# First attention layer: scores of two heads side by side in two 64-row tiles, and values projected with standing weights

## The reference

```python
# NH = 32 query heads, KVH = 8 key/value heads, GROUPS = 4, HD = 16
q = hidden @ Wq + bq;  k = ctx @ Wk + bk;  v = ctx @ Wv + bv
scores = einsum('bkgld,bksd->bkgls', q, k) * HD ** -0.5 + mask
attn = softmax(scores);  out = einsum('bkgls,bksd->bkgld', attn, v)
x = layer_norm(out @ Wo + bo + hidden) * gamma + beta
# then two cross-attention layers of 16 heads of 128, and an MLP of 2048
```

## Time and profile before

| | us |
|---|---|
| median of 3 runs | 2617.61 |
| lowest, highest | 2616.01, 2618.43 |
| profiled execution, first to last instruction | 2614.3 |
| loop of the first layer, batch 0 (38.59 to 282.59) | 244.0 |
| loop of the first layer, batch 1 (1337.68 to 1581.70) | 244.0 |

### The profile page before, as it was taken

One profiled execution on the slowest core, in us unless ns is written; L12 is line 12 of the kernel. 1 busy time (PEld: TensorE's weight loads), 2 busy tenths in 40 slices (PEclk: granted clock), 3 DMA queues, 4 the chain that ended last, 5 costly groups with the idle time before them and its releaser, 6 DMA issues.

```text
span 2614.3 us, 48985 instructions
## 1 busy us (share of the span) xinstructions
PE 2580.6 (99%) x17560; PEld 2145.5 (82%) x17560; DVE 1730.6 (66%) x2636; ACT 1504.9 (58%) x2356; POOL 1311.1 (50%) x746
## 2 busy tenths in 40 slices
PE   8999999999999999999999999999999999999999
PEld 6777788888888888888877777888888888888887
DVE  7999775656657666665279996665666576666541
ACT  5999555555545555545459994555554455554543
POOL 1244246666543666654613432466655546665644
PEclk9999999999999999999999999999999999999999
DMA  7312025345322435442472110344544143553521
GB/s 202 101 51 68 34 68 130 99 115 134 104 75 76 122 98 126 128 103 80 153 154 83 54 65 33 90 108 110 130 113 120 53 99 99 125 129 102 131 72 65
DMA packets 88386, 261.81 MB, mean 100 GB/s; under 512 B 20112, under 2 KB 33696, under 8 KB 81840
## 3 DMA queue, kind: packets, MB, share of 16 engines
q1 hardware_dynamic: 86336, 258.83, 37.3%
q10 hardware_dynamic: 1904, 0.98, 0.2%
HBM read 135.45 MB, written 6.83 MB: 54 GB/s over the span
## 4 chain that ended last, share of the span: by engine, by line
PE 88%; DVE 4%; issue 2%; ACT 2%; DMA 2%; POOL 1%; SPq 1%; DVEq 0%; POOLq 0%; ACTq 0%
PE ps_m L1059 21%; PE ps_t L1059 18%; PE ps_s L1059 15%; PE ps_m L1316 6%; PE ps_t L1316 6%; PE ps_t L1191 6%; PE ps_m L1206 5%; PE ps_s L1175 4%; PE ps_m L1191 3%; POOL pT_lo L524 1%; SPq L442 1%; PE ps_m L1249 1%; PE ps_m L1069 1%; DMA pT_lo<-pb 1%; ACT p L850 1%
## 5 line engine op out<-in xcount | busy, mean ns | idle before, releaser
L524 POOL TENSOR_TENSOR pT_lo<-pT_lo,pT_hi 128x1024 fp32r<-128x1024 f32 x220 | 529.2, 2406 | 501.7 <-ACT pT_hi L710 496.4
L710 ACT ACTIVATE pT_hi<-pT_lo 128x1024 fp32r<-128x1024 f32 x224 | 237.8, 1061 | 327.6 <-DMA pT_lo<-pb 327.6
L850 ACT ACTIVATE p<-ps_s,nm 128x1024 f32<-128x1024 f32 x256 | 284.7, 1112 | 203.4 <-DVE nm L1752 202.7
L1749 DVE TENSOR_REDUCE nmx<-ps_s 128x1 f32<-128x1024 f32 x256 | 309.7, 1210 | 121.6 <-PE ps_s L1059 121.6
L1059 PE MATMUL ps_s<-kT,qT 128*128 128x512 f32 x1536 | 383.9, 392 | 0.1
L1768 DVE STREAM_TRANSPOSE pb<-p 128x1024 f32<-128x1024 f32 x224 | 278.1, 1242 | 106.2 <-ACT p L850 101.7
L1059 PEld LDWEIGHTS ps_s<-kT,qT 128*128 128x128 f32 x1536 | 281.3, 188 | 55.6 <-ACT p L850 1.0
L1674 DVE CUSTOM_DVE_ANT_0 sm<-ps_s,mask 128x1024 f32<-128x1024 f32 x256 | 309.7, 1211 | 5.6 <-ACT p L804 2.2
L804 ACT ACTIVATE p<-sm,nm 128x1024 f32<-128x1024 f32 x256 | 293.7, 1147 | 33.3 <-DVE nm L1674 30.7
L1059 PE MATMUL ps_t<-ctxT,wa 128*128 128x512 f32 x1080 | 256.0, 390 | 0.0
L1059 PE MATMUL ps_m<-hT,wa 128*128 128x512 f32 x1008 | 243.7, 393 | 0.7 <-ACT g L1021 0.7
(11 more groups left out here) (176 smaller groups left out, 4671.7 us busy)
## 6 DMA issues: line engine op xcount, KB each, us to landing
pT_lo<-pb SPq DMA_DIRECT2D x896, 128.0 KB, 2.3
stg_qk<-in_wqk SPq DMA_DIRECT2D x40, 1024.0 KB, 7.5
stg_vo<-in_wo SPq DMA_DIRECT2D x48, 512.0 KB, 3.5
wob<-in_wo SPq DMA_DIRECT2D x32, 512.0 KB, 3.6
stg_vo<-in_wv SPq DMA_DIRECT2D x32, 512.0 KB, 3.6
q_stack<-scr_q SPq DMA_DIRECT2D x48, 128.0 KB, 4.2
st_ctx<-in_ctxT SPq DMA_DIRECT2D x8, 512.0 KB, 6.6
bv_row<-scr_bv SPq DMA_DIRECT2D x32, 128.0 KB, 5.7
```

What stands on the lines that cost most here:

```text
L524: return nc.gpsimd.tensor_tensor(out, x, f32(hi), ALU.subtract)
L710: return nc.scalar.activation(out, in_, ACT.Copy)
L850: nc.scalar.activation(p[t % 2][:], ps_s[t % 2][:], ACT.Exp, bias=nm[:, i:i + 1], scale=SCALE1, accum_out=sums[:, i:i + 1]).then_inc(exp_d ...
L1749: nc.vector.tensor_reduce(nmx[:, i:i + 1], ps_s[t % 2][:], AX.X, ALU.max, negate=True)\
```

## The change

Scores: keys and queries are now kept as two float32r parts, 48 rows for a head instead of 96. Two heads lie in one stack, at rows 0 to 47 and 64 to 111, and `scores0(r)` makes steps 2r and 2r+1 together: four matmuls of 512 columns, two for each bank of `ps_s`, alternating between the two tiles. It waits for the maxima of both steps before. The loops of TensorE, ACT and VectorE go by pairs of steps. The two heads of a pair belong to different key/value heads; `v32` gets a third block of 16 columns, and `w0o` another order of rows. VectorE makes one low part instead of three operations with two bfloat16 parts. Values: `add_v` projects them as the keys, with the weights stationary and 512 tokens moving, 24 matmuls per batch; ACT adds the bias into `vT0`, TensorE turns it in eight transposes, and VectorE copies it to `v32` in two copies.

```diff
-Q_ORDER = (0, 0, 1, 1, 0, 2)
-K_ORDER = (0, 1, 0, 1, 2, 0)
+Q_ORDER = (0, 0, 1)
+K_ORDER = (0, 1, 0)
+TILE = 64
+PAIRS0 = STEPS0 // 2
-        v32 = sb("v32", [P, ST, KVH, 2 * HD], F32)
+        v32 = sb("v32", [P, ST, KVH, 3 * HD], F32)
-        bank_of_half = [h % 2 if h < 2 * UNIT else h % 3 for h in range(2 * STEPS0)]
+        bank_of_half = [h % 2 if h < 2 * UNIT else (0, 1, 2, 0, 2, 1, 0, 2)[h % 8] for h in range(2 * STEPS0)]
...
@@ scalar, set-up
+                for i in range(2):
+                    act.wait_ge(v0_filled, 2 * b + i + 1)
+                    nc.scalar.activation(vT0[:, i * 512:(i + 1) * 512], ps_t[i][:], ACT.Identity, scale=1.0,
+                                         bias=cols0[:, 5:6]).then_inc(v0_biased, 1)
                 for k in range(2):
                     act.wait_ge(scr_k_out[k], 16 * (b + 1))
-                    stack_k(act, k, slice(0, 2), stack_in)
+                    stack_k(act, k, slice(0, 1), stack_in)
@@ scalar, loop
-                for t in range(STEPS0):
+                for t in range(1, STEPS0, 2):
+                    copied0(t - 1, 0)
                     copied0(t, 0)
                     if t + 2 < STEPS0:
+                        exp0(t + 1)
                         exp0(t + 2)
@@ tensor, set-up
                 for c in range(CT):
                     pe.wait_ge(in_hi, b * (CT + 2) + 1 + c + 1)
-                    for i in range(2):
-                        add_k(i, c, 0, 0, start=c == 0)
-                        add_k(i, c, 1, 0)
+                    for add in (add_k, add_v):
+                        for i in range(2):
+                            add(i, c, 0, 0, start=c == 0)
+                            add(i, c, 1, 0)
...
-                project_v0(0)
+                finish_v(0)
...
                 project_q0(0)
-                for i in range(1, 4):
-                    project_v0(i)
...
+                finish_v(1)
...
+                for i in range(2):
+                    pe.wait_ge(v0_biased, 2 * b + i + 1)
+                    for s in range(4):
+                        st = 4 * i + s
+                        mm = nc.tensor.transpose(ps_t[i][:, s * P:(s + 1) * P], vT0[:, st * P:(st + 1) * P], ident[:])
+                    mm.then_inc(v0_turned, 1)
@@ tensor, loop
+                def scores0(r):
+                    kp, lt = divmod(2 * r // UNIT, LT)
+                    if r >= 1:
+                        pe.wait_ge(max0_done, t0 + 2 * r)
                     for n in range(2):
+                        for e in range(2):
+                            rows = slice(TILE * e, TILE * e + STACK)
+                            mm = nc.tensor.matmul(ps_s[e][:, n * 512:(n + 1) * 512],
+                                                  q_stack[rows, kp * GROUPS + r % GROUPS, lt * P:(lt + 1) * P],
+                                                  k_stack[rows, kp, n * 512:(n + 1) * 512],
+                                                  start=True, stop=True)
+                            if n == 1:
+                                mm.then_inc(s0_filled, 1)
...
-                for t in range(1, STEPS0):
+                for r in range(1, PAIRS0):
+                    t = 2 * r + 1
...
+                    if r + 1 < PAIRS0:
+                        scores0(r + 1)
+                    turned0(t - 1)
                     turned0(t)
...
-                    if t >= GROUPS and t % 2 == 1:
+                    if t >= GROUPS:
                         for i in (t % GROUPS - 1, t % GROUPS):
                             values0(t // GROUPS * GROUPS - GROUPS, i)
@@ vector, set-up
+                def low_part(i):
+                    dve.wait_ge(wide_done, b * 6 + i + 1)
+                    apart()
+                    nc.vector.scalar_tensor_tensor(out=parts[i % 3][:, 1, :], in0=ps_m[i % 2][:], scalar=column0(i),
+                                                   in1=f32(parts[i % 3][:, 0, :]), op0=ALU.add, op1=sub)\
+                        .then_inc(part_done, 1)
...
@@ vector, loop
-                for t in range(STEPS0):
+                for t in range(1, STEPS0, 2):
...
                     if t + 2 < STEPS0:
+                        maxima0(t + 1)
                         maxima0(t + 2)
+                    copied0(t - 1, 1)
                     copied0(t, 1)
...
-                    if t % UNIT == GROUPS and t > UNIT:
+                    if t % UNIT == GROUPS + 1 and t > UNIT:
                         normalised(t // UNIT - 1)
```

More of the change, by code:

```diff
@@ L136, in build @@
         at[0] += 128
-        q_stack = sb("q_stack", [STACK, NH0, L], BF16)
-        k_stack = sb("k_stack", [STACK, KVH, S], BF16)
-        v32 = sb("v32", [P, ST, KVH, 2 * HD], F32)
+        q_stack = sb("q_stack", [P, NH0 // 2, L], F32R)
+        k_stack = sb("k_stack", [P, KVP, S], F32R)
+        v32 = sb("v32", [P, ST, KVH, 3 * HD], F32)
         mask = sb("mask", [P, LT, S], F32)
@@ L344, in turned_bank, with stack_rows, stack_k @@
             return ps_s[c // 2][:, c % 2 * 512:(c % 2 + 1) * 512]
-        def stack_k(engine, i, kvs, done):
+        def stack_rows(e, j):
+            return slice(TILE * e + HD * j, TILE * e + HD * j + HD)
+        def stack_k(engine, i, kps, done):
             for j in range(len(K_ORDER)):
-                src = scr_k[i, :, K_ORDER[j], :].rearrange("(a e) n -> e a n", e=HD)
-                engine.dma_start(k_stack[HD * j:HD * j + HD, kvs, i * 512:(i + 1) * 512], src[:, kvs, :])\
-                    .then_inc(done, 16)
+                src = scr_k[i, :, K_ORDER[j], :].rearrange("(k e d) n -> e d k n", e=2, d=HD)
+                for e in range(2):
+                    engine.dma_start(f32(k_stack[stack_rows(e, j), kps, i * 512:(i + 1) * 512]), src[e][:, kps, :])\
+                        .then_inc(done, 16)
         @block.sync
@@ L400, in stack_q @@
                     for j in range(len(Q_ORDER)):
-                        src = scr_q[i, :, Q_ORDER[j], :].rearrange("(a e) n -> e a n", e=HD)
-                        sp.dma_start(q_stack[HD * j:HD * j + HD, i * 8:(i + 1) * 8, :], src).then_inc(done, 16)
+                        src = scr_q[i, :, Q_ORDER[j], :].rearrange("(e g d) n -> e d g n", e=2, d=HD)
+                        for e in range(2):
+                            sp.dma_start(f32(q_stack[stack_rows(e, j), i * GROUPS:(i + 1) * GROUPS, :]), src[e])\
+                                .then_inc(done, 16)
                 sp.dma_start(mask[:, 1:, :], d["mask"][b, :, 1:, :]).then_inc(mask_rest, 16)
@@ L762, in wide @@
                                      bias=column0(i)).then_inc(wide_done, 1)
-            for dst, name in ((cols, "cols"), (cols0, "cols0"), (colf, "colf"), (lnc, "lnc"), (bv0, "bv0"),
-                              (bvr, "bv")):
-                src = d[name]
-                act.dma_start(dst[:], src.partition_broadcast(P) if name == "bv0" else src).then_inc(const_in, 16)
+            for dst, name in ((cols0, "cols0"), (cols, "cols"), (colf, "colf"), (lnc, "lnc"), (bvr, "bv")):
+                act.dma_start(dst[:], d[name]).then_inc(const_in, 16)
             hi_kv(0)
@@ L1151, in _ @@
                 project_q0(0)
-                for i in range(1, 4):
-                    project_v0(i)
-                for i in range(1, 3):
-                    pe.wait_ge(w0q_lo, CT * b + i + 1)
-                    project_q0(i)
+                finish_v(1)
+                pe.wait_ge(w0q_lo, CT * b + 2)
+                project_q0(1)
+                for i in range(2):
[4 more added lines that the diff above has]
+                    mm.then_inc(v0_turned, 1)
@@ L1159, in _ @@
+                pe.wait_ge(w0q_lo, CT * b + 3)
+                project_q0(2)
                 pe.wait_ge(stack_in, 16 * 18 * (b + 1))
[L1160 to L1161 removed]
+                pe.wait_ge(v32_done, b * 3 + 3)
                 apart()
                 t0, u0, g0 = b * STEPS0, b * UNITS0, b * (STEPS0 // GROUPS)
[L1166 to L1168 removed]
@@ L1170, in scores0 @@
-                def scores0(t):
-                    kv, lt, gr = place(t)
-                    if t >= 2:
-                        pe.wait_ge(max0_done, t0 + t - 1)
-                    for n in range(2):
-                        mm = nc.tensor.matmul(ps_s[t % 2][:, n * 512:(n + 1) * 512],
-                                              q_stack[:, kv * GROUPS + gr, lt * P:(lt + 1) * P],
-                                              k_stack[:, kv, n * 512:(n + 1) * 512],
-                                              start=True, stop=True)
-                    mm.then_inc(s0_filled, 1)
+                def scores0(r):
+                    kp, lt = divmod(2 * r // UNIT, LT)
+                    if r >= 1:
+                        pe.wait_ge(max0_done, t0 + 2 * r)
+                    for n in range(2):
+                        for e in range(2):
+                            rows = slice(TILE * e, TILE * e + STACK)
[5 more added lines that the diff above has]
+                                mm.then_inc(s0_filled, 1)
```

(10 more changed lines are left out.)

109 lines of the change are left out of this document (36 added, 73 removed).

## The result

The changed kernel takes 2692.11 us (median of 4 runs, 2689.71 to 2694.15), the kernel before beside it 2616.97: ratio 1.0287, 95% interval 1.0272 to 1.0301. It is slower, inside the range I gave, but by 75 us where I had said 48. Three of the runs further down had one execution far above its others (3245, 8986 and 3608 us), which their times and ratios leave out.

What follows compares the result with a forecast made beforehand. The prediction took TensorE to set the pace (3.80 us per pair). Its terms, 2614.3 + 50.6 (loop) - 2.5 (set-up) = 2662.4, plus 3.3 for the median, gave 2666 us, 1.8% slower; 8-in-10 range 2632 to 2714.

Steps and rivals of the forecast that it cites:

- The wait at each unit's start: First-layer loop: TensorE's products wait for VectorE's later normalisation; pair 5.82 us against 3.69, unit 17.0 against 15.2.
- The round of 3.69 by ACT: Ordinary pairs: exponential, turning, copy, exponential take 3.69 us, above TensorE's 3.55 and VectorE's 3.50.
- The loop's opening: Start of the first layer's loop: two small VectorE operations instead of six, 1 us less per batch.
- its 15 waits: Loop: 15 of 16 units per batch have the wait for the normalisation, +1.78 us each, +26.7 per batch.
- the first unit: Loop, first of 16 units per batch: has no wait and saves 0.4 us.
- The set-up: Before the loop: scores 2 to 3 us earlier in batch 0, 0 in batch 1; -2.5 us in all.
- The tiles: Scores on TensorE: two tiles work side by side, four matmuls take 0.5 us, within bounds of 0.44 and 0.88.
- The dear change: TensorE's ordinary pair: a tiling change at the full drain price of 0.42 us makes it 3.82, sum some 12 us higher.
- the tiles don't overlap: Rival on scores: tiles served in turn, TensorE's pair 3.99, unit 18.3, time 2707 us; chance 0.09.
- The short wait: Rival at unit starts: VectorE has only the last copy left, unit 15.9, time 2633 us; chance 0.14.
- the case in which nothing moves: Rival for the whole kernel: short wait, 3.69 round and good set-up cancel, 2612 to 2623 us; chance 0.06.
- The faster case: Rival at unit starts: normalisation ends in time, unit 14.9, time 2602 us; chance 0.07.

Runs made afterwards that it cites:

- the first experiment: Changed kernel with VectorE's normalisation moved between the two maxima of its pair instead of behind both copies; 2625.19 us, ratio 1.0025.
- all three orders: Changed kernel with normalisation between maxima, first eight steps' even copy before the second maximum, ACT alternating copies and exponentials, keys' products first; 2614.33 us, ratio 0.9984.

## Why the prediction was right in direction and short in size

- **The wait at each unit's start: right.** 17.0 us per unit said, 17.00 measured in 25 of the 28 distances between full units and 18.50 in three. Inside, the waiting pair is 5.75 (said 5.82), an ordinary pair 3.66 (3.69), and the turning of the inverses 0.26 (0.11); these cancel. The 0.11 was right for the kernel before, where full turning follows it; now it stands between the narrow products and the tiled scores, and 0.15 more is most likely one more change of the array's division. The three long units stand where the clock had fallen, 0.87 from 150 to 160 us, and add 4.5 us that I hadn't counted.
- **The round of 3.69 by ACT: right number, wrong reason.** ACT's order can be changed without moving the pair. It is TensorE's 3.55, as I had said, and 0.12 of waiting for a half bank.
- **The loop's opening: the step that failed.** I said "and I give back 1 us" because four VectorE operations fewer stand there. It costs 8.6 and 9.2 us instead, some 7 us each without the later place. I had priced the pairs' order by the steady loop with its three half banks; in the first eight steps there are two, so that the turning of a pair's second step waits for VectorE's copy of the first, and in the new order two maxima stand ahead of it. The line with `bank_of_half` was in the diff. With its neighbour, first scores to first maximum at low clock (0.6 each), it is +19.0 us for both batches. Of these 3.5 are the later place of the normalisation, which the sum had among its 15 waits; that leaves 15.5 where the sum had -2.8 (1 for the opening and 0.4 for the first unit, twice). So the opening has 18.3 of the 29.8 us by which the profiled execution is longer than my sum; the set-up has 5.8, the three long units 4.5, what lies behind the loop 2.1, and -0.9 is left over.
- **The set-up: wrong sign.** Said -2.5 and 0, measured +2.3 and +1.0. VectorE's shorter work and the smaller total on TensorE didn't help. TensorE now idles 2.2 us ahead of the queries' group, and in this execution the clock was low behind it (4.60 us for twelve matmuls against 3.04 in a run with the same gap). So the size of the +2.3 is partly luck: where the same set-up ran at full clock, the scores began at 37.07 and 37.57, 0.2 to 0.7 us earlier than before, still not the 2 to 3 I had expected. And loads of the stacks land last in any case: with the keys first and a write of `scr_q` at 23.42 us the scores began at 36.96, while before a write at 27.45 gave 37.80.
- **The tiles: right.** I took 0.5 us for the scores and 0.15 for a further change; 0.67 was measured for both. The Trainium skill, "TensorEngine Tiling (Array Packing)", section Key Properties, says that tiles operate independently, and that a change of mode drains TensorE. The rows agree with the first (0.67 against 1.13 in one tile). The dear change that I had priced from it, an ordinary pair of 3.82, is not there: the pair is 3.66.
- **Rivals.** That the tiles don't overlap fell with the run in one tile. The short wait didn't come about, nor the case in which nothing moves. The faster case, the normalisation in time, is what the first experiment builds: its unit is 14.91 where I had said 14.9, and its time 2625 where I had said 2602, again for the opening and the set-up.
- **The clock.** I took it as full throughout, as the earlier trace rows had it. Behind gaps on TensorE there are now stretches at the lower of its two levels (1.2 GHz), and the change made many gaps.

## What to carry to other kernels

Before going from single steps to pairs, list for each queue which instruction now stands between a result and the one that waits for it; one of 0.28 us that stood behind two copies and a maximum cost 67 us here. Price the start of a loop by its own buffers: where it has fewer of them than the steady part, an order that is free later isn't free there. And take work off the bounding engine only after looking at what would be late next: here 0.44 us of scores per pair became 0.12, since three half banks and a copy on ACT stood right behind.

## What the runs showed of the hardware

- Four float32r matmuls of 48 rows and 512 columns over two row tiles take the same 0.67 us whether they alternate between the tiles or go tile by tile; in a single tile they take 1.13.
- TensorE's granted clock falls behind gaps that before weren't there: 0.68 from 50 to 60 us in the changed kernel, 0.66 in the set-up of batch 1 with all three orders, 1.00 with transposes in the gap. It doesn't fall behind each: the same set-up with the same gap of 2.2 us was seen at 0.83 and at 1.00 from 20 to 30 us in kernels that differ only behind it, 2.5 us apart at the first scores. The Trainium skill, "TensorE: Matmul & The Clock Gate", section Part 1, has the low level as the default that activity releases. Batch 1 of the run with idle transposes agrees, 1.00 against 0.66.
- Two ACT copies of 256 columns last 0.66 us together, one of 512 columns 0.60.
- The Trainium skill, "TensorEngine Tiling (Array Packing)", section PSUM Bottleneck, says that tiling speeds up TensorE but not the copies out of PSUM. Here the rows agree: the pair's last transposes start 0.05 us behind the end of ACT's 0.60 us copy out of PSUM, and a copy longer by 0.06 made the pair longer by 0.06.
